# Shifting the tiles of a six-stage transformer kernel to one remainder by 512 bytes, and reordering its last stage

## The reference

```
x = layernorm(x + attention_0(x))            # 32 query heads, 8 key/value heads, width 128
x = layernorm(x + channel_attention_0(x, ctx))
x = layernorm(x + ffn_0(x))                  # int4 weights with scales, 512 -> 1792 -> 512
x = layernorm(x + attention_1(x))            # ALiBi
x = layernorm(x + cross_attention_1(x, ctx)) # keys and values from ctx, RMS norm of q and k
x = layernorm(x + ffn_1(x))                  # the last stage, below
```

```
base = xf @ W_base.T + b_base
gate = softmax(xf @ W_gate.T)                     # 8 experts
thr  = sigmoid(xf @ W_thr + b_thr) * 0.125
w    = (gate - thr) * (gate - thr >= 0);  w = w / sum(w)   (sum 0 -> 1)
h    = einsum('nd,erd->ner', xf, A_w)             # 8 x 16 hidden values per token
out  = base + 2 * einsum('ner,ne,eor->no', h, w, B_w)
```

## Time and profile before

| | |
|---|---|
| runs (3) | 2502.17, 2505.59, 2510.26 us; median 2505.59 |
| the profiled execution | 2508.61 us, of which the span from the first to the last instruction is 2506.8 |
| TensorE busy in the span | 2412.6 us (96%) |
| VectorE, ScalarE, GpSimd busy | 1198.5, 787.2 and 738.8 us |
| mean granted TensorE clock | 0.962 of full speed (2.4 GHz) |

### The profile page before, as it was taken

The page is one execution under the profiler, slowest core; times in us unless marked ns, Lnnn a source line. Parts: engine busy times, 40 slices in busy tenths (PEclk is TensorE's granted clock), DMA queues, the critical chain, the costliest instruction groups (busy, mean ns, idle before and its releaser), DMA issues.

```text
span 2506.8 us, 35240 instructions
## 1 busy us (share of the span) xinstructions
PE 2412.6 (96%) x12594; PEld 1927.3 (77%) x12594; DVE 1198.5 (48%) x2215; ACT 787.2 (31%) x1512; POOL 738.8 (29%) x686
## 2 busy tenths in 40 slices
PE   8999999999999989998999999999899999999987
PEld 6888888876555557776788888887788888888876
DVE  2444443447777753435343444445345444543565
ACT  2222222223666652221322222222133233322220
POOL 4122212203222226444322122211444333333232
PEclk9999999998999999999999999999789999999989
DMA  4111111100000033220201111110111011101000
GB/s 136 43 39 38 38 38 42 33 18 11 15 11 15 10 113 125 78 73 25 70 27 35 38 42 40 38 31 1 56 43 39 18 33 38 42 21 33 17 30 34
DMA packets 51409, 101.84 MB, mean 41 GB/s; under 512 B 8592, under 2 KB 11152, under 8 KB 50832
## 3 DMA queue, kind: packets, MB, share of 16 engines
q1 hardware_dynamic: 51344, 100.97, 12.7%
HBM read 98.85 MB, written 2.10 MB: 40 GB/s over the span
## 4 chain that ended last, share of the span: by engine, by line
PE 81%; DVE 7%; issue 6%; POOL 3%; ACT 2%; DMA 0%; DVEq 0%; POOLq 0%; ACTq 0%; SPq 0%
PE pb L257 21%; PE pb L259 19%; PE pb L258 19%; PE pb L528 7%; PE pb L581 4%; PE pb L540 2%; PE pb L1092 2%; PE pb L1106 2%; PE pb L568 2%; POOL f_wl L1540 1%; PE pb L1073 1%; POOL f_il L1548 1%; PE pb L1080 1%; DVE x_kmx L1250 1%; DVE x_qmx L1259 1%
## 5 line engine op out<-in xcount | busy, mean ns | idle before, releaser
L257 PE MATMUL pb<-xTh,wh 128*128 128x512 f32 x1024 | 424.6, 415 | 10.0 <-DVE xTl L1800 8.6
L259 PE MATMUL pb<-xTh,wl 128*128 128x512 f32 x1024 | 409.2, 400 | 0.0
L258 PE MATMUL pb<-xTl,wh 128*128 128x512 f32 x1024 | 408.8, 399 | 0.0
L823 DVE TENSOR_TENSOR X<-pb,X 128x512 f32<-128x512 f32 x192 | 132.8, 692 | 415.7 <-PE pb L259 415.6
L257 PE MATMUL pb<-woh,oth 128*128 128x512 f32 x768 | 322.6, 420 | 0.3
L258 PE MATMUL pb<-wol,oth 128*128 128x512 f32 x768 | 307.9, 401 | 0.0
L259 PE MATMUL pb<-woh,otl 128*128 128x512 f32 x768 | 307.6, 400 | 0.0
L893 POOL TENSOR_TENSOR sc_sb<-sc_sb,rs 128x512 f32<-128x512 f32 x96 | 100.0, 1045 | 678.1 <-DVE rs L790 678.1
L657 ACT ACTIVATE q_sb<-pb 128x512 f32<-128x512 f32 x192 | 114.6, 597 | 434.3 <-PE pb L259 434.3
L257 PEld LDWEIGHTS pb<-xTh,wh 128*128 128x128 f32 x1024 | 196.2, 192 | 52.8 <-issue 10.4
L259 PEld LDWEIGHTS pb<-xTh,wl 128*128 128x128 f32 x1024 | 195.0, 190 | 48.1
(11 more groups left out here) (209 smaller groups left out, 4218.3 us busy)
## 6 DMA issues: line engine op xcount, KB each, us to landing
raw<-in_a_in SPq DMA_DIRECT2D x144, 256.0 KB, 2.7
raw<-in_a_out SPq DMA_DIRECT2D x96, 256.0 KB, 2.6
f_q<-in_f_q SPq DMA_DIRECT2D x21, 512.0 KB, 3.9
f_s<-in_f_s SPq DMA_DIRECT2D x21, 512.0 KB, 5.4
X<-in_x SPq DMA_DIRECT2D x1, 2048.0 KB, 10.9
x_craw<-in_ctx SPq DMA_DIRECT2D x8, 256.0 KB, 2.6
x_ct<-in_ctxT_pair SPq DMA_DIRECT2D x16, 128.0 KB, 2.1
f_c<-in_ctxT SPq DMA_DIRECT2D x2, 1024.0 KB, 5.1
```

Of the source, the lines that this page charges most:

```text
L257: nc.tensor.matmul(out, w_hi, x_hi, start=start, stop=False)
L258: nc.tensor.matmul(out, w_hi, x_lo, start=False, stop=False)
L259: return nc.tensor.matmul(out, w_lo, x_hi, start=False, stop=stop)
L823: nc.vector.tensor_tensor(xtile(n), bank[:, :], xtile(n), ALU.add).then_inc(A["x_added"], 1)
```

## The change

It has two parts.

**Placement.** `onecol` becomes 16 columns wide (64 bytes in place of 32), of which column 0 is used. With that, the stages' own tiles start at byte 99,456, with the remainder 128. `g_raw`, `g_h` and `g_l` are padded from 3,112 to 3,200 columns, so `g_h` and `g_l` have the remainder 128 too. All rounded tiles now have 128 but `g_zh` and `g_zl`, which have 288. No instruction's shape is changed by this part, except that the memset of `onecol` writes 16 columns.

**The last stage.** The gate products (`pe_gate`, into the banks 2 and 4) of the tiles 0 to 3 are issued within the tail of the cross attention: 0 and 1 ahead of the transpose of tile 6, 2 and 3 ahead of the transpose of tile 7. Their eviction is split: VectorE copies 10 columns of logits (`dve_logits`), then ScalarE 128 hidden columns (`act_hidden`). `weigh`, the transposes, the rounding to `g_zh` and `low_z` go by groups of four tiles in place of single tiles, and `g_zh`, `g_zl` hold all eight tiles. TensorE's order after the gates is base 0 to 2, transposes of group 0, base 3, transposes of group 1, experts 0 to 2, base 4, experts 3 and 4, then base and experts of 5, 6 and 7. Each tile has its own PSUM bank.

```diff
-        onecol = keep("onecol", [P, 1])
+        onecol = keep("onecol", [P, 16])
...
+            GW = (NGW + 127) // 128 * 128
-            g_raw = sb("g_raw", [P, NGW])
-            g_h = sb("g_h", [P, NGW], F32R)
-            g_l = sb("g_l", [P, NGW], F32R)
+            g_raw = sb("g_raw", [P, GW])
+            g_h = sb("g_h", [P, GW], F32R)
+            g_l = sb("g_l", [P, GW], F32R)
...
-            g_hid = sb("g_hid", [P, NT, GC])
+            g_hid = sb("g_hid", [P, NT, E_ * R_])
+            g_lg = sb("g_lg", [P, NT, E_ + 2])
...
-            g_zh = sb("g_zh", [P, 2, P], F32R)
-            g_zl = sb("g_zl", [P, 2, P], F32R)
+            g_zh = sb("g_zh", [P, NT, P], F32R)
+            g_zl = sb("g_zl", [P, NT, P], F32R)
...
+            if st.name == "xattn1":
+                pe.wait_ge(gs["w"], 2)
+                for t in range(2):
+                    pe_gate(pe, t)
             if st.name != "attn0":
-                for t in (NT - 2, NT - 1):
-                    pe_transpose_tile(pe, st.name, t, pb[t % 2], st.unit_read(NKV, -1))
+                pe_transpose_tile(pe, st.name, NT - 2, pb[0], st.unit_read(NKV, -1))
+            if st.name == "xattn1":
+                for t in range(2, 4):
+                    pe_gate(pe, t)
+            if st.name != "attn0":
+                pe_transpose_tile(pe, st.name, NT - 1, pb[1], st.unit_read(NKV, -1))
...
+            if st.name == "xattn1":
+                for t in range(2):
+                    act_hidden(act, t)
             if st.name != "attn0":
-                for t in (NT - 2, NT - 1):
-                    act_transpose_tile(act, st.name, t, pb[t % 2])
+                act_transpose_tile(act, st.name, NT - 2, pb[0])
+            if st.name == "xattn1":
+                for t in range(2, 4):
+                    act_hidden(act, t)
+            if st.name != "attn0":
+                act_transpose_tile(act, st.name, NT - 1, pb[1])
...
+            if st.name == "xattn1":
+                dve_logits(dve, 0)
             dve_normalise(dve, st.name, NT - 1, xtile(NT - 1), xtile(NT - 1))
+            if st.name == "xattn1":
+                dve_logits(dve, 1)
             if st.name != "attn0":
-                for t in (NT - 2, NT - 1):
-                    dve_transpose_tile(dve, st.name, t, pb[t % 2])
+                dve_transpose_tile(dve, st.name, NT - 2, pb[0])
+            if st.name == "xattn1":
+                for t in range(2, 4):
+                    dve_logits(dve, t)
+            if st.name != "attn0":
+                dve_transpose_tile(dve, st.name, NT - 1, pb[1])
...
+        GATE = (pb[2], pb[4])
+
+        def dve_logits(dve, t):
+            dve.wait_ge(gs["p1"], t + 1)
+            nc.vector.tensor_copy(g_lg[:, t, :], GATE[t % 2][:, E_ * R_:GC]
+                                  ).then_inc(gs["ev"], 1)
+
+        def act_hidden(act, t):
+            act.wait_ge(gs["ev"], t + 1)
+            nc.scalar.activation(g_hid[:, t, :], GATE[t % 2][:, 0:E_ * R_], ACT.Copy).then_inc(gs["hd"], 1)
+
+        def pe_gate(pe, t):
+            h = slice(t * P, (t + 1) * P)
+            pe.wait_ge(xt_ready, 24 + t + 1)
+            if t >= 2:
+                pe.wait_ge(gs["hd"], t - 1)
+            for k in range(KT):
+                last = mm3(GATE[t % 2][:, 0:2 * P], (xTh[:, k, h], xTl[:, k, h]),
+                           (g_part(g_h, k, "gate"), g_part(g_l, k, "gate")), k == 0, k == KT - 1)
+            last.then_inc(gs["p1"], 1)
...
+                if t == 0:
+                    pe.wait_ge(xt_ready, 24 + NT)
+                if t == 2:
+                    pe.wait_ge(gs["hd"], NT)
                 if t >= 6:
-                    pe.wait_ge(ln_bn, 8 * LN_NORMS["ffn1"] + t - 5)
+                    pe.wait_ge(gs["zr"], t - 5)
...
+            def transpose(n):
+                pe.wait_ge(gs["z"], n + 1)
+                for m in range(4):
+                    last = nc.tensor.transpose(pb[6 + n][:, m * P:(m + 1) * P], g_z[:, 4 * n + m, :], ident[:, :])
+                last.then_inc(gs["zt"], 1)
...
-            for t in range(NT):
-                first(t)
+            for t in range(4, NT):
+                pe_gate(pe, t)
             pe.wait_ge(gs["w"], len(G_PARTS))
-            for t in range(6):
+            for t in range(3):
                 base(t)
             transpose(0)
+            base(3)
             transpose(1)
-            for t in range(NT):
+            for t in range(3):
                 experts(t)
-                if t + 2 < NT:
-                    transpose(t + 2)
-                if 2 <= t < 4:
-                    base(t + 4)
+            base(4)
+            experts(3)
+            experts(4)
+            for t in range(5, NT):
+                base(t)
+                experts(t)
```

More of the change, by code:

```diff
@@ L539, in square_sums @@
                 for m in range(8):
-                    last = nc.tensor.matmul(pb[3][:, m:m + 1], sq[:, m, :], onecol[:, :], start=True, stop=True)
+                    last = nc.tensor.matmul(pb[3][:, m:m + 1], sq[:, m, :], onecol[:, 0:1], start=True, stop=True)
                 last.then_inc(A["ss_done"], 1)
@@ L1594, in g_part @@
                 return tile[:, KT * DM + k * GC:KT * DM + k * GC + 2 * P]
-            return tile[:, KT * DM + KT * GC:]
+            return tile[:, KT * DM + KT * GC:NGW]
         def sp_ffn1(sp):
@@ L1665, in route, with weigh, low_z @@
                 link(nc.vector.tensor_tensor(g_wn[:, :, :], g_w[:, :, :], spread(g_wr[:, :], E_), ALU.mult))
-            def weigh(t):
+            def weigh(n):
+                rows = slice(4 * n, 4 * n + 4)
+                dve.wait_ge(gs["hd"], 4 * n + 4)
                 nc.vector.scalar_tensor_tensor(
-                    g_z[:, t, :].rearrange("p (e r) -> p e r", e=E_),
-                    g_hid[:, t, 0:NG].rearrange("p (e r) -> p e r", e=E_), 2.0,
-                    g_wn[:, t, :].rearrange("p (e o) -> p e o", o=1).to_broadcast([P, E_, R_]),
+                    g_z[:, rows, :].rearrange("p t (e r) -> p (t e) r", e=E_),
+                    g_hid[:, rows, :].rearrange("p t (e r) -> p (t e) r", e=E_), 2.0,
+                    g_wn[:, rows, :].rearrange("p t (e o) -> p (t e) o", o=1).to_broadcast([P, 4 * E_, R_]),
                     ALU.mult, ALU.mult).then_inc(gs["z"], 1)
[L1675 to L1678, removed]
+            def low_z(n):
+                dve.wait_ge(gs["zhi"], n + 1)
+                nc.vector.tensor_tensor(g_zl[:, 4 * n:4 * n + 4, :], pb[6 + n][:, :].rearrange("p (t n) -> p t n", t=4),
+                                        f32(g_zh[:, 4 * n:4 * n + 4, :]), ALU.subtract).then_inc(gs["zr"], 1)
             def finish(t):
@@ L1689, in emit @@
                 dve_normalise(dve, "ffn1", t, xtile(t), g_o[:, t % 4, :])
-            for t in range(NT):
-                dve.wait_ge(gs["p1"], t + 1)
-                nc.vector.tensor_copy(g_hid[:, t, :], pb[6 + t % 2][:, 0:GC]).then_inc(gs["ev"], 1)
+            for t in range(4, NT):
+                dve_logits(dve, t)
             dve.wait_ge(gs["ev"], NT)
             route()
-            for t in range(NT):
-                weigh(t)
+            weigh(0)
+            weigh(1)
             low_z(0)
@@ L1706, in dve_ffn1 @@
             emit(NT - 1)
-        def pe_ffn1(pe):
[L1709 to L1717, removed]
+        GATE = (pb[2], pb[4])
@@ L1733, in experts @@
             def experts(t):
-                pe.wait_ge(gs["zr"], t + 1)
-                mm3(pb[t % 6][:, :], (g_zh[:, t % 2, :], g_zl[:, t % 2, :]),
+                pe.wait_ge(gs["zr"], t // 4 + 1)
+                mm3(pb[t][:, :], (g_zh[:, t, :], g_zl[:, t, :]),
                     (g_part(g_h, 0, "up"), g_part(g_l, 0, "up")), False, True).then_inc(gs["p2"], 1)
             pe.wait_ge(A["x_added"], 192)
-            pe.wait_ge(gs["w"], 2)
-            for t in range(NT):
-                first(t)
+            for t in range(4, NT):
+                pe_gate(pe, t)
@@ L1754, in act_ffn1 @@
+            for t in range(5, NT):
+                base(t)
+                experts(t)
         def act_ffn1(act):
+            for t in range(4, NT):
+                act_hidden(act, t)
             act.wait_ge(gs["res"], 1)
             nc.scalar.activation(g_e[:, :, :], g_e[:, :, :], ACT.Exp).then_inc(gs["exp"], 1)
[L1757 to L1761, removed]
+            for n in range(2):
+                act.wait_ge(gs["zt"], n + 1)
+                nc.scalar.activation(g_zh[:, 4 * n:4 * n + 4, :], pb[6 + n][:, :].rearrange("p (t n) -> p t n", t=4),
+                                     ACT.Copy).then_inc(gs["zhi"], 1)
```

20 lines of the change are left out of this document (8 added, 12 removed).

## The result

| | before | after |
|---|---|---|
| median of 4 runs each | 2505.74 us | 2473.09 us (2471.99 to 2474.11) |
| ratio, 95% interval | | 0.9864 (0.9849 to 0.9879) |
| profiled execution, its span | 2508.61, 2506.8 us | 2473.64, 2471.8 us |
| mean granted clock | 0.962 | 0.965 |
| start of the last matmul of the last output projection | 2446.4 us | 2424.4 us |

The kernel is faster by 1.4%, 32.7 us by the medians; the prediction said 2470. Between the profiled executions it is 35.0 us: 22.0 ahead of the end of the last output projection, 13.0 behind it.

A forecast was written before the change was run, and what follows sets the result against it. TensorE, busy 96% of the span, was taken to bound the kernel. 2508.6 - 20 (placement) - 12.2 (last stage) - 4.7 (clock) = 2471.7, or 2469 by the median, stated as 2470 us; 8-in-10 range 2450 to 2497.

The forecast's parts named there:

- The difference decides, at 0.2267 when it is zero: TensorE's 512-column matmuls: the difference of both operands' remainders sets the pitch, settling at 0.2267 us without one; whole forecast's chance 0.67.
- the moving tile's own remainder decides: Rival on matmul pitch: moving tile at 96 is good, 128 bad; 10 us dearer, time 2503; chance 0.07.
- placement does nothing: Rival: the two pitch levels come from something else, only the last stage gains; time 2493; chance 0.14.
- equal remainders of 128 are the worst: Rival: each of 6384 matmuls goes to 0.24 us, 53 us dearer, time 2546; chance 0.04.
- Way in of the first ffn, 4.5 us: First ffn's input matmuls: 3 lines x 224, each 0.0067 us shorter, 4.5 us off.
- Projections, 13.2 us: Attention projections: 3 x 1024 matmuls gain 0.0046 us each, 14.1 us, less 6% for the lower clock, 13.2.
- The approach that vanishes, 3.0 us: Some 90 output runs directly after input runs: slow approach after a placement switch vanishes, 0.037 us each, near 3.0 us.
- Key/value units, 1.5 us: Cross attention's 3 x 256 matmuls of 256 columns: bounds 0 and 0.004 us gain each, half taken, 1.5 us.
- Part one in sum: Placement's terms together, with 2 us taken off for waits in the first ffn: 20 us, bounds 0 and 30.
- The clock, -4.7 us: Cross attention steps: effect on stretches at 1.2 GHz not readable; middle taken near one long step fewer, -4.7 us.
- The last stage, 12.2 us: Kernel's end: early gates and grouped tiles fill TensorE's waits, 10.8 + 1.4 = 12.2 us, bounds 5 and 14.
- The fourth rival: Last stage gives its lower bound, clock goes the wrong way, placement as forecast: 2490, taken as 2486; chance 0.08.

The follow-up runs named there:

- the probes: Two separate kernels, TensorE alone issuing stretches of 96 matmuls at set operand offsets; 226.67 to 234.29 ns for 512 columns, 113.31 to 120.00 for 256.
- e7: Kernel after with a filler ahead of all tiles, kept and stage tiles at remainder 96 instead of 128; 2471.87 us, ratio 0.9861.
- e10: Kernel after with a wider filler, stage tiles 64 bytes above the kept ones; 2493.89 us, ratio 0.9945.
- e11: Kernel after with a wider filler, stage tiles 256 bytes above the kept ones; 2472.33 us, ratio 0.9865.
- e9: Kernel after with the two context tiles moved 64 bytes above the others; median 2480.76 us, ratio 0.9892.
- e1: Kernel before with the placement part alone, last stage as before; 2485.30 us, ratio 0.9908.
- e2: Kernel after without the placement, so the reordered last stage alone; 2493.74 us, ratio 0.9945.
- e3: Kernel after with gates 0 to 3 and their evictions moved back behind the transpose of tile 7; 2476.51 us, ratio 0.9873.
- e5: Kernel after, unchanged, measured again; 2471.92 us, ratio 0.9864.
- e6: Kernel after with the two context tiles at remainder 96, all others at 128; median 2463.30 us, ratio 0.9858.
- the first probe: Separate kernel, TensorE alone: 26 stretches of 96 matmuls at set operand offsets; for 512 columns 226.67 ns at difference 0, 233.33 at 32 bytes.

## Why the prediction was right, point by point

- **The difference decides, at 0.2267 when it is zero.** Shown for 512 columns, by the probes, e7, e10 and e11. For 256 columns it isn't the whole of it (two levels in e9). The rival that the moving tile's own remainder decides falls with them, the rival that placement does nothing with e1 (22.3 us), and the one that equal remainders of 128 are the worst with the changed kernel itself. By the Trainium skill, "SBUF — State Buffer", section "Who interferes with whom", TensorE's two read ports are independent, one for the moving operand and one for the weight load. The runs differ from the reading that the pitch then has no reason to depend on the places: for one shape, with no other engine at work, the pitch goes from 226.7 to 234.3 ns with nothing but the distance of the two operands.
- **Way in of the first ffn, 4.5 us.** In pitch it arrived: 659 matmuls at 2.4 GHz go from 233.4 to 226.8, 4.3 us. In time it didn't. The stage takes 261.2 us before and 261.0 after (windows of TensorE, the kernel before first):

```profile
923.70:1184.90 261.20, 244.62 (x1047) 0.98 0.23 81
```

```profile
918.80:1179.80 261.00, 242.90 (x1047) 0.97 0.23 81
```

  TensorE is busy 1.7 us less and idle 1.5 us more. The stretches at 1.2 GHz add up to 16.4 us in place of 10.1, which costs half of 6.3, 3.1 us. And TensorE waits longer for GpSimd's rest of the weights. The chain of waits, before and after:

```profile
PE pb L257 <- POOL f_wl L1540: 4.1, 5, 2.5
```

```profile
PE pb L259 <- POOL f_wl L1565: 5.7, 5, 3.5
```

  The 2 us that I took off for "not all of it arrives" named this place; of the stage's whole gain in pitch all but 0.2 us is gone. Both losses go with the pitch. In the three traces at the old pitch (before, e2, e10) the stretch from the ffn's first matmul to its last has 3.4 us at 1.2 GHz and waits 4.1 us for the rest of the weights; in all eight at the new one it has 10.2 to 13.6 and waits 5.2 to 5.7. How the shorter pitch brings more time at 1.2 GHz is open.
- **Projections, 13.2 us.** Mis-sized: 2802 matmuls at 2.4 GHz from 233.17 to 229.24 ns make 11.0. The pitch fell by 3.9 ns, not by 4.6. In the kernel after, runs that go on from an output projection have 226.7, those behind scores 229.8, behind transposes of the probabilities 230.3 and behind products with values 232.7, for they approach 226.7 only at their end.
- **The approach that vanishes, 3.0 us.** The approach did vanish: where an output projection follows a projection unit directly, the mean pitch goes from 229.4 to 226.7 ns, some 2.5 us over 77 runs. But output projections behind a burst of products with values got dearer by 1.8 ns, from 229.6 to 231.3, which the prediction had no term for. Over all output projections it is 229.57 to 228.87, 1.4 us, and 0.3 on the way out of the ffn: 1.7 in place of 3.0.
- **Key/value units, 1.5 us.** Wrong in sign. No row had such a pair without a difference, and I took half of the gain of 512 columns. It is 118.2 to 119.7, 1.1 us dearer, and the probe shows why the bounds were wrong: for 256 columns zero is among the dearest differences (120.00, against 118.33 at 32). The bounds should have gone below nothing.
- **Part one in sum.** By pitch 11.0 + 4.3 + 1.4 + 0.3 (way out) - 1.1 = 15.9 us, against 20 with the 2 taken off. e1's 22.3 contain more clock: its stretches at 1.2 GHz add up to 180.9 us in place of 192.0, another 5.5.
- **The clock, -4.7 us.** The sign was right, and it was a guess. Up to the last output projection the stretches at 1.2 GHz went from 184 to 171 us; half of the difference is 7 us. The other traces point to the placement: 178 and 184 us in e2 and e10 at the old pitch, 167 to 174 in e1, e3, e5, e7 and e11, one execution each. It came in another form than forecast: no step went from long to short; five of six are now 78.6. "Short steps near 76.4" was wrong for this kernel, though e6 has 76.80. With this, the part ahead of the last stage is 15.9 + 7 - 1.6 (the longer wait) = 21.3, against the 22.0 read from the two traces and the 24.7 forecast.
- **The last stage, 12.2 us.** It gave 13.0, and 12.6 in e2. Gates: forecast 12.9 us behind the last output projection, measured 12.7; the transpose of tile 6 forecast 3.3 us behind it and found there at 2427.91; that of tile 7 forecast 6.7 and found 6.6, at 2431.20. e3 shows the gates' 5.2 by themselves. No idle of over 0.5 us between the first base and the last expert, and the last sum at once behind the last matmul: both hold. By windows from 2446.67 and 2424.63 on, the gates gave 5.8 us (18.48 to 12.70), the bases and experts 5.3 (33.95 to 28.62; 4.5 of it waits) and what follows the last matmul 1.85 (7.70 to 5.85), where 5.2, 5.6 and 1.4 were forecast.
- **The time.** Against the profiled execution the sum was 2471.7, and 2473.6 came: 2.7 us too much ahead of the last stage, 0.8 too little in it. That it came so close is in part luck. The placement was forecast at 20 us and gave 14.3 by pitch and waits, and the clock, a guess, made up for 2.3 of that.
- **Sums of the prediction that don't hold.** The 6384 matmuls in the upper bound are the projections, the output projections and both ways of the ffn; the bases aren't among them. The fourth rival comes out at 2490 by its own sum, and the 2486 that was taken has no working.

## What to carry to other kernels

Of a matmul with a new stationary operand each time, measure the pitch against the distance of the two operands, for the column count that is used, before tiles are placed: 0, 16, 240, 256 and 272 bytes were best for 512 columns here and 64 either way for 256 columns, and a filler of 32 bytes moved 1%. Then measure it again in the kernel: at 64 bytes the units of 256 columns didn't hold the level of the probe. In the first ffn a gain of 4.3 us in pitch was not paid out, so read a gain again per stage, with its waits and its clock, from the trace after. Where a row is missing for a shape, let its bounds reach below nothing.

## What I had not expected of the hardware

- The pitch of 512-column matmuls takes values between 226.67 and 234.29 ns in the probes by the difference of the two addresses, 256-column ones between 113.31 and 120.00, and the orders of the differences are not the same. +16 and -16 bytes differ (226.67, 228.33), as do +64 and -64 (233.33, 228.88).
- The level is not reached at once. In the first probe the stretch at difference 256 begins with pitches of 228, 232 and 231 ns before it stays at 227, and many runs of 12 in the kernel end before they have settled.
- One difference can have two levels. In e9 runs of 24 and 48 matmuls of 256 columns keep either 113.3 or 117.8 ns to their end, and e10, at -64, has only 117.8 where the probe has 113.3.
- One and the same kernel, e9, took 2462.96 us at a mean clock of 0.969 and 2483.73 at 0.961. The eight executions of the changed kernel, which differs from it by addresses alone, lie within 3 us. The chip isn't the reason as far as is seen: e6, with the same spread, ran on the one of e5.
